# A transformer layer's front: parts, row loads and early projections dealt anew over the engines, the first rows loaded in three stages

## What is computed

```python
def _layernorm(x, axis=-1, eps=1e-05):
    m = jnp.mean(x, axis=axis, keepdims=True)
    v = jnp.var(x, axis=axis, keepdims=True)
    return (x - m) / jnp.sqrt(v + eps)
...
        q = x @ Wq.T + bq
        k = x @ Wk.T + bk
        v = x @ Wv.T + bv
...
        q, k, v = (split(q), split(k), split(v))
        scores = jnp.einsum('bhqd,bhkd->bhqk', q, k) / jnp.sqrt(jnp.float32(HEAD_DIM))
        if CAUSAL:
            mask = jnp.tril(jnp.ones((seq, seq), bool))
            scores = jnp.where(mask, scores, jnp.float32(NEG))
        attn = jax.nn.softmax(scores, axis=-1)
        out = jnp.einsum('bhqk,bhkd->bhqd', attn, v)
        out = out.transpose(0, 2, 1, 3).reshape(batch, seq, D_MODEL)
        return out @ Wo.T + bo
...
        logits = x @ gate_w.T
        top_v = jnp.max(logits, axis=-1)
        sel = jnp.argmax(logits, axis=-1)
        rw = jax.nn.sigmoid(top_v)
        out = jnp.zeros_like(x)
        n_exp = gate_w.shape[0]
        for e in range(n_exp):
            mask = (sel == e).astype(x.dtype)
            xs = x * (rw * mask)[:, None]
            g = xs @ w_gate[e].T
            u = xs @ w_up[e].T
            out = out + u * jax.nn.silu(g) @ w_down[e].T
        return out.reshape(b, s, h)
    x = L0_attn_x
    x = x + _L0_attn_ref(_layernorm(x, axis=-1), ...)
    x = x + _L0_ffn_ref(_layernorm(x, axis=-1), ...)
    return x
```

## Time and profile before

| | before |
|---|---|
| median of 3 runs (lowest to highest) | 519.79 us (519.75 to 520.91) |
| the profiled execution | 519.78 us, span 518.1 |
| busy share of the span | PE 95%, DVE 85%, ACT 73%, POOL 44% |
| granted TensorE clock, mean | 0.989 |
| first lead piece, first turn, first score product of unit 0 | 31.90, 43.65, 58.25 us |

### The profile page before, as it was taken

The page is one execution under the profiler, slowest core; times in us unless marked ns, Lnnn a source line. Parts: engine busy times, 40 slices in busy tenths (PEclk is TensorE's granted clock), DMA queues, the critical chain, the costliest instruction groups (busy, mean ns, idle before and its releaser), DMA issues.

```text
span 518.1 us, 12773 instructions
## 1 busy us (share of the span) xinstructions
PE 493.8 (95%) x4797; PEld 219.9 (42%) x4797; DVE 442.3 (85%) x695; ACT 375.8 (73%) x790; POOL 225.5 (44%) x526
## 2 busy tenths in 40 slices
PE   8699799999999999999999999999999999999997
PEld 7555333243333324333343333334332346777764
DVE  5958789999999999999999989999998358888864
ACT  7245598988889888898988889898888972223321
POOL 5398165363544536344463634446244242222200
PEclk9899999999999999999999999999999999999999
DMA  6251023323202341220234112021130212222001
GB/s 176 48 149 63 4 66 73 101 65 101 73 7 74 84 103 53 48 74 8 75 85 108 50 29 76 10 76 41 46 95 7 74 42 67 61 63 62 20 22 40
DMA packets 33550, 32.63 MB, mean 63 GB/s; under 512 B 10448, under 2 KB 26960, under 8 KB 33488
## 3 DMA queue, kind: packets, MB, share of 16 engines
q1 hardware_dynamic: 33376, 31.48, 23.0%
q10 hardware_dynamic: 112, 0.33, 0.2%
HBM read 20.26 MB, written 11.01 MB: 60 GB/s over the span
## 4 chain that ended last, share of the span: by engine, by line
PE 62%; DVE 28%; ACT 4%; POOL 3%; issue 2%; ACTq 0%; POOLq 0%; DVEq 0%
PE ps L1201 19%; DVE top_p L900 10%; PE ps L1185 10%; PE ps L1146 8%; DVE top_p L895 7%; DVE top_p L897 6%; PE ps L1268 6%; PE ps L1254 5%; PE ps L1259 5%; POOL xn L574 2%; ACT sum_sb L769 2%; DVE top L916 2%; PE ps L1154 1%; PE ps L1230 1%; ACT prob L778 1%
## 5 line engine op out<-in xcount | busy, mean ns | idle before, releaser
L778 ACT ACTIVATE prob<-ps 128x512 f32<-128x512 f32 (+2 forms) x640 | 303.4, 564 | 33.4 <-PE ps L1185 32.2
L655 POOL TENSOR_SCALAR_AFFINE_SELECT prob<-prob 128x256 f32<-128x256 f32 x256 | 99.6, 416 | 176.9 <-ACT prob L778 173.9
L1185 PE MATMUL ps<-q_rows,k_rows 51*128 51x512 bf16 (+3 forms) x768 | 169.7, 329 | 1.2 <-ACT gate_x L733 1.0
L895 DVE TENSOR_REDUCE top_p<-ps 128x2 f32<-128x1024 f32 x128 | 151.0, 1221 | 9.6 <-PE ps L1146 8.6
L1201 PE MATMUL ps<-prob,v_all 128*9 128x512 f32 (+3 forms) x1536 | 157.7, 491 | 1.4 <-POOL prob L655 0.2
L1146 PE MATMUL ps<-k_rows,q_rows 48*128 48x128 bf16 (+3 forms) x1024 | 113.7, 266 | 7.5 <-DVE top_p L900 4.4
L1185 PEld LDWEIGHTS ps<-q_rows,k_rows 51*128 51x128 bf16 x768 | 53.4, 94 | 145.5 <-ACT prob L778 128.1
L900 DVE TENSOR_REDUCE top_p<-ps 128x8 f32<-128x1024 f32 x64 | 76.7, 1220 | 10.8 <-PE ps L1154 10.3
L897 DVE TENSOR_REDUCE top_p<-ps 128x4 f32<-128x1024 f32 x64 | 75.4, 1216 | 2.7 <-PE ps L1146 2.7
L1146 PEld LDWEIGHTS ps<-k_rows,q_rows 48*128 48x128 bf16 x1024 | 45.6, 94 | 27.0 <-DVE top_p L900 8.9
L1201 PEld LDWEIGHTS ps<-prob,v_all 128*9 128x9 f32 x1536 | 24.5, 88 | 51.5 <-issue 30.9
(11 more groups left out here) (110 smaller groups left out, 453.4 us busy)
## 6 DMA issues: line engine op xcount, KB each, us to landing
split_parts<-part SPq DMA_DIRECT2D x12, 384.0 KB, 4.4
q_rows<-split_parts SPq DMA_DIRECT2D x31, 96.0 KB
k_rows<-split_parts SPq DMA_DIRECT2D x31, 96.0 KB
value_sums<-sum_sb SPq DMA_DIRECT2D x128, 18.0 KB
x_sb<-x SPq DMA_DIRECT2D x8, 256.0 KB, 4.5
qk<-value_sums SPq DMA_DIRECT2D x8, 256.0 KB, 3.8
qk<-inverse_sums SPq DMA_DIRECT2D x8, 256.0 KB, 4.1
out<-y SPq DMA_DIRECT2D x8, 256.0 KB, 2.3
```

The lines of the kernel that those rows point to most:

```text
L655: last = g.affine_select(out=quarter, in_=quarter, pattern=[[0, GH], [1, Q]], base=Q * (1 - z), channel_multiplier=-1, compare_op=ALU.is_g ...
L778: a.activation(prob[:, i % NB, g0:g0 + heads, 0:cols], ps[:, load_at(u, n) % 3, 0:heads * cols].rearrange("p (s t) -> p s t", s=heads), AC ...
L895: return v.tensor_reduce(top_p[:, c, place, s:s + 3:2, m], banks, AX.X, ALU.max)
L1185: last = mm(ps[:, l % 3, m * cols:(m + 1) * cols], k_rows[rows, k, j // TPH, s + m, j % TPH * P:(j % TPH + 1) * P], q_rows[rows, k, c, s + ...
```

## The change

- ScalarE casts part 0 of half (0,1), DVE makes both halves' third parts, and GpSimd none.
- Unit 0's parts leave one by one, twelve stores in place of four (`send_first`), each part with a semaphore of its own (`first_out`).
- Unit 0's rows are loaded in three stages (`load_first`): stage 0 (the q rows of part 0 in three copies, and the k rows with one part) on GpSimd's queue, once part 0 has landed; stage 1 on SyncE; stage 2 on SyncE and ScalarE, two DMAs each.
- xn of half (1,0) goes from DVE to ScalarE, as x times rstd plus a shift (minus mean times rstd) that GpSimd computes.
- xn_t of (1,1), v of (1,0), q and k of (1,1) are copied out of PSUM by DVE in place of ScalarE; steps 6 and 7 are measured after that.
- GpSimd raises rstd of steps 6 and 7 after it has scaled batch 2; its memset of v_all stands earlier, that of ramp later.
- The bias products stand in the front between two runs of `keep_busy` (12 and 12 in place of 36) and read b_v and b_oc broadcast in place.
- `AHEAD` is 8: v of (1,1) stands before the first piece.

```diff
@@ -121,7 +121,7 @@
     EARLY += [("v", *half)] if half == (1, 1) or not after else [("xn_t", *after), ("v", *half)]
     if half == (1, 1):
         EARLY.append(("xn_t", *after))
-AHEAD = 7
+AHEAD = 8
...
+        def load_first(eng, n, rg):
+
+            loaded = rows_in[0] if n else first_in
+            load_queries(eng, 0, rg, *PART_ROWS[n], loaded)
+            load_keys(eng, 0, rg, *PART_ROWS[2 - n], loaded)
+
+        def rows_loaded(u):
+
+            return 192 * (u // 3 + 1) - (0 if u % 3 else 64)
 
...
@@ -392,10 +410,17 @@
...
+            def send_first(h, n0, n1):
+                for s in range(2):
+                    for n in range(n0, n1):
+                        sp.dma_start(split[:, n, 0:1, :, :, h, s, :].rearrange("e u d r t -> (u d r) e t"),
+                                     part[64 * s:64 * s + 16, h, :, n, :]).then_inc(first_out[n], 16)
+
...
@@ -410,17 +435,32 @@
...
-            for h in range(2):
-                send_parts(0, h, range(0, 1))
-            for h in range(2):
-                sp.wait_ge(split_out[h], 32)
+            sp.wait_ge(first_part[0], 1)
+            send_first(0, 0, 1)
+            sp.wait_ge(first_part[1], 1)
+            send_first(1, 0, 1)
+            sp.wait_ge(first_part[0], 2)
+            send_first(0, 1, 2)
+            sp.wait_ge(part3_set[0], 1)
+            send_first(0, 2, 3)
+            sp.wait_ge(first_part[1], 2)
+            send_first(1, 1, 2)
+            sp.wait_ge(part3_set[1], 1)
+            send_first(1, 2, 3)
             sp.wait_ge(k_rows_set, 1)
-            load_rows(0)
-            sp.wait_ge(rows_in[0], 192)
+
+            for n in range(2):
+                sp.wait_ge(first_out[n], 64)
+            load_first(sp, 1, 0)
+            load_first(sp, 1, 1)
+            sp.wait_ge(first_out[2], 64)
+            load_first(sp, 2, 0)
+            sp.wait_ge(first_in, 64)
+            sp.wait_ge(rows_in[0], rows_loaded(0))
             for h in range(2):
                 send_parts(0, h, range(1, UPB))
             for h in range(2):
-                sp.wait_ge(split_out[h], 64)
+                sp.wait_ge(split_out[h], 32)
             load_rows(1)
             send_top(0, 0)
...
@@ -554,16 +594,16 @@
...
+            g.memset(v_all[:, :, :, :, HD:HD + 1], 1.0).then_inc(v_ones_set, 1)
             rsqrt1(2, 2)
-            pool.wait_ge(part2_set, 1)
-            g.tensor_tensor(part[:, 0, :, 2, :], rest[:, 0, :, :], part[:, 0, :, 1, :],
-                            ALU.subtract).then_inc(part3_set[0], 1)
-            g.memset(v_all[:, :, :, :, HD:HD + 1], 1.0).then_inc(v_ones_set, 1)
-            for e in range(EXPERTS):
-                last = g.memset(ramp[:, :, e:e + 1], float(EXPERTS - e))
-            last.then_inc(const_set, 2)
+            pool.wait_ge(rstd_set, 3)
+            chain.link(g.tensor_tensor(shift[:], moments1[:, 2, :, 0], rstd1[:, 2, :], ALU.mult))
+            g.tensor_scalar(shift[:], shift[:], -1.0, None, ALU.mult).then_inc(shift_set, 1)
+            pool.wait_ge(k_rows_set, 1)
+            pool.wait_ge(first_out[0], 64)
+            load_first(g, 0, 0)
+            load_first(g, 0, 1)
             rsqrt1(4, 2)
-            rsqrt1(6, 2)
...
             scale(2)
+            rsqrt1(6, 2)
             scale(3)
...
+            for e in range(EXPERTS):
+                last = g.memset(ramp[:, :, e:e + 1], float(EXPERTS - e))
+            last.then_inc(const_set, 2)
             split_top(0, 0)
...
@@ -746,6 +790,8 @@
             for h in range(2):
                 copy_side(0, h, 0)
                 copy_side(0, h, 1)
+            act.wait_ge(qk_set[1], 2)
+            a.activation(part[:, 1, :, 0, :], qk[:, 0, 1, :, :], ACT.Copy).then_inc(first_part[1], 1)
             act.wait_ge(centre_mm, 1)
             a.activation(w_v[:, DIM:], ps[:, 0, 0:EXPERTS], ACT.Copy).then_inc(w_v_set, 1)
...
@@ -754,13 +800,20 @@
...
-            for e in EARLY[:1]:
+            act.wait_ge(shift_set, 1)
+            act.wait_ge(turned[0], 1)
+            for i in range(TPH):
+                last = a.activation(xn[:, 0, i, :], x_sb[:, 2 * TPH + i, :], ACT.Identity,
+                                    bias=shift[:, i:i + 1], scale=rstd1[:, 2, i:i + 1])
+            last.then_inc(xn_set[0], 1)
+            for e in EARLY[:3]:
                 take(e)
-            for h in range(2):
-                act.wait_ge(split_out[h], 32)
             act.wait_ge(k_rows_set, 1)
-            load_half(act, 0, 1, PART_ROWS[:2])
-            for e in EARLY[1:]:
+            for n in range(3):
+                act.wait_ge(first_out[n], 64)
+            load_first(act, 2, 1)
+
+            for e in EARLY[7:]:
                 take(e)
...
@@ -847,44 +900,74 @@
...
             def take_parts(h):
                 dve.wait_ge(qk_set[h], 2)
-                chain.link(v.tensor_copy(part[:, h, :, 0, :], qk[:, 0, h, :, :]))
+                if h == 0:
+                    v.tensor_copy(part[:, h, :, 0, :], qk[:, 0, h, :, :]).then_inc(first_part[h], 1)
+                dve.wait_ge(first_part[h], 1)
                 chain.link(v.tensor_tensor(rest[:, h, :, :], qk[:, 0, h, :, :], part[:, h, :, 0, :],
                                            ALU.subtract))
-                second = v.tensor_copy(part[:, h, :, 1, :], rest[:, h, :, :])
-                if h == 0:
-                    second.then_inc(part2_set, 1)
-                else:
-                    chain.link(second)
-                    v.tensor_tensor(part[:, h, :, 2, :], rest[:, h, :, :], part[:, h, :, 1, :],
-                                    ALU.subtract).then_inc(part3_set[h], 1)
+                v.tensor_copy(part[:, h, :, 1, :], rest[:, h, :, :]).then_inc(first_part[h], 1)
+                dve.wait_ge(first_part[h], 2)
+                v.tensor_tensor(part[:, h, :, 2, :], rest[:, h, :, :], part[:, h, :, 1, :],
+                                ALU.subtract).then_inc(part3_set[h], 1)
 
...
             measure(2)
             measure(3)
             take_parts(0)
             take_parts(1)
-            scale(1, 0)
-            scale(1, 1)
-            dve.wait_ge(bias_in, 16 * 4)
-            v.tensor_copy(xs[:, 0, 0, :], b_v[:].to_broadcast((P, DIM)))
-            v.tensor_copy(xs[:, 0, 1, :], b_oc[:].to_broadcast((P, DIM))).then_inc(wide_set, 1)
-            for n in range(4, STEPS):
-                measure(n)
+            scale(3)
+            dve.wait_ge(bias_mm, 1)
+            v.tensor_tensor(b_o[:], b_o[:], ps[:, 4, 0:DIM], ALU.add)
+            v.tensor_copy(b_gate[:], ps[:, 4, DIM:WIDE]).then_inc(bias_set, 1)
+
+            def copy_side(b, h, side):
+                dve.wait_ge((q_mm, k_mm)[side][h], b + 1)
+                v.tensor_scalar(qk[:, b, h, side, :], ps[:, 1 + side, :], b_qk[:, side:side + 1], None, ALU.add
+                                ).then_inc(qk_set[h], 1)
+
+            def copy_xn(b, h):
+                dve.wait_ge(turned[h], b + 1)
+                dve.wait_ge(v_mm[h], b)
+                tokens = xn_t[:, h, :].rearrange("p (m e t) -> p m e t", e=2, t=Q)
+                v.tensor_copy(tokens[:, :, 1, :], ps[:, 0, 0:HALF // 2].rearrange("p (m t) -> p m t", t=Q))
+                v.tensor_copy(tokens[:, ::-1, 0, :], ps[:, 0, HALF // 2:].rearrange("p (m t) -> p m t", t=Q)
+                              ).then_inc(xn_t_set[h], 1)
+
+            def copy_v(b, h):
+                dve.wait_ge(v_mm[h], b + 1)
+                at = wide(v_banks(b, h))
+                tile = b * (2 * TPH) + h * TPH
+                for z in range(2):
+                    v.tensor_copy(v_all[:, b, h * TPH + 2 * z:h * TPH + 2 * z + 2, :, 0:HD],
+                                  at[:, z, :, 0:DIM].rearrange("p j (g d) -> p j g d", d=HD))
+                v.tensor_copy(gate_x[:, tile:tile + TPH, :].rearrange("p (z j) e -> p z j e", z=2), at[:, :, :, DIM:]
+                              ).then_inc(v_set[h], 1)
+
+
+            assert EARLY[3:7] == [("xn_t", 1, 1), ("v", 1, 0), ("q", 1, 1), ("k", 1, 1)]
+            measure(4)
+            measure(5)
+            copy_xn(1, 1)
+            copy_v(1, 0)
+            copy_side(1, 1, 0)
+            copy_side(1, 1, 1)
+            measure(6)
+            measure(7)
             dve.wait_ge(top_low_set, 1)
 
...
@@ -939,10 +1022,6 @@
             for e in LEAD:
                 if e[0] in ("piece", "turn"):
                     take(e)
-                if e == ("piece", 0, 0):
-                    dve.wait_ge(bias_mm, 1)
-                    v.tensor_tensor(b_o[:], b_o[:], ps[:, 1, 0:DIM], ALU.add)
-                    v.tensor_copy(b_gate[:], ps[:, 1, DIM:WIDE]).then_inc(bias_set, 1)
...
@@ -1092,8 +1171,6 @@
                     turn1(b, h, 0).then_inc(turned[h], 1)
                 elif kind == "q":
                     pe.wait_ge(qk_set[1 - h if n else 0], 2 * (b + h) - 1)
-                    if n == 2:
-                        pe.wait_ge(bias_set, 1)
...
@@ -1115,13 +1192,21 @@
             project_v(0, 1).then_inc(v_mm[1], 1)
```

(13 more changed lines are left out.)

60 lines of the change are left out of this document (30 added, 30 removed).

## The result

The changed kernel takes 517.16 us, the median of six runs (516.05 to 519.34), beside 519.83 (519.35 to 520.91) for the kernel before, run beside it: a ratio of 0.995, with a 95% interval of 0.9934 to 0.9967. That is 2.7 us less; 3.0 were forecast, and 516.8 us. The profiled execution took 516.74 us, with a span of 515.0.

The account below looks back on a forecast made before the run. The prediction took GpSimd's gapless row before the first turn, then TensorE's serial list to S, as the bound on unit 0's start. Terms -1.9, -1.4 and +0.3 sum to -3.0: 516.8 us, range 514.9 to 518.8.

Parts of the forecast that it names:

- the two large terms: Unit 0's start: the first turn 1.9 us earlier, and the list from that turn to S 1.4 us shorter.
- DVE's head: DVE's steps before GpSimd's first raise: both halves in 7.15 us, ending at 19.8, so GpSimd starts at 23.8.
- S: TensorE's first score matmul of unit 0, at 58.25 us before the change, forecast at 55.0.
- GpSimd's row sets the turn: GpSimd's raises, 16 scalings, memsets and split before TensorE's first turn: turn at 41.8 instead of 43.65, -1.9 us.
- The DMAs on GpSimd's queue: Four row-load issues before GpSimd's first raise: 1.1 us each, covered by 5.1 us of waiting, zero in the sum.
- rivals 1 and 2: GpSimd's DMAs delay the head: 1, up to 7.1 us, 523.9 (chance 0.11); 2, partial slip, 517.4 to 518.8 (0.16).
- AHEAD = 8: TensorE between turn and S: one projection (1.06 us) moves before the turn, last piece (0.32) fills a wait; -1.4 us.
- Given back in unit 0: Behind S: the last piece's reduction and join on DVE end later, delaying TensorE's next piece; +0.3 us.
- TensorE's front: TensorE before the turn: first piece at 29.5, DVE's reductions done at 39.9, under 41.8; staged loads pay zero.
- 3 (DVE sets the turn): If GpSimd's scalings took 0.65 instead of 0.78, DVE's 39.9 would set the turn: 514.9 us; chance 0.07.
- 4 (the clock stays low in the front): TensorE's first piece comes 2 us later, moments 6 and 7 are 0.7 late for GpSimd: 517.5 us; chance 0.09.
- 5 (no shift survives): The first units swallow the shift, held by a store or load of SyncE's: 519.5 us; chance 0.07.

Follow-up runs that it names:

- The second group of runs: The changed kernel run once more, unaltered, beside its variants and the kernel before: 517.69 us over nine runs, ratio 0.9949.
- ScalarE's scaling: Changed kernel with xn of half (2,0) made by ScalarE instead of GpSimd and the ramp memsets behind the split: 514.88 us, ratio 0.9902.
- the three kernels with late rows: Changed kernel with unit 0's old stores and row loads (519.33 us), the same with 36 useless products before the first piece (516.84), or stage 0 on SyncE (518.91).
- the two kernels with fill: Changed kernel with useless products in three idle places of unit 0 (516.65 us), and that with 24 more ahead of the first turn (515.04).
- the old loads: Changed kernel with unit 0's parts in four stores and rows loaded by SyncE (eight DMAs) and ScalarE (four), none by GpSimd: 519.33 us, ratio 0.9979.

## Why the prediction was right, and where not

The mechanism was right for the two large terms. That the number came out so close is in part luck. In the profiled execution 0.4 us of scatter at the start and 0.4 us more than worked out in DVE's head stand against 0.6 us more given back behind S. The second group of runs has 2.3 us instead of 2.7. And the medians of the changed kernel hold time at half clock that no term priced.

**GpSimd's row sets the turn: right.** Forecast 18.0 us from its first raise to the turn, measured 17.96; the half microsecond put in front of the split came out at the turn as 0.47.

**DVE's head: right, a little better than worked out.** The cast came at 12.21 and its steps for the two halves ended at 19.28, so 7.07 for the 7.15 of the sum; the parts of 1.22 and 1.23 are in the table to 0.01. The rest up to GpSimd's start was 3.8 instead of 4.0. What made the difference of 3.04 long, GpSimd's subtraction beside it, is shown by the run that gives GpSimd its subtraction back: 3.08. The shares of ScalarE's cast and of the four scalings rest on rows alone.

**The DMAs on GpSimd's queue: right that they are covered; the size was below the value taken.** Bounds 1.2 to 12.2 us for the four, taken 4.4, measured 0.84 + 0.56 + 0.60 + 0.54 = 2.5, begun at 19.11 where 18.7 was worked out, and 1.39 us of cover left. The first two stood beside DVE's four scalings (19.20 to 20.31) and show nothing of the 3.06 that I allowed. In the second execution of the changed kernel they began at 17.78, beside DVE's cast and subtraction, and took 0.84, 0.56, 0.60 and 0.68. And the kernel without these four starts its raise at the same time. So rivals 1 and 2 fall. What the Trainium skill states (SBUF — State Buffer, section on SBUF's two separate sides), 3100 ns for such a DMA overlapped with DVE, is not borne out here: the issues took 0.54 to 0.84 us, and the whole of one, issue to landing, 2.7 to 2.8 in the profiled execution. The page speaks of a DVE copy in a two-port mode, and no run here tells whether these DVE steps hold the port as that one does.

**AHEAD = 8: right.** 13.22 us from the turn to S (13.2 forecast), and 14.60 with `AHEAD` at 7. This holds at full clock: 14.80 and 15.30 were seen in executions whose clock fell behind the turn. It holds too only while TensorE waits for GpSimd at the turn, as the prediction has it: where it reaches the turn without a wait, it waits 0.47 or 0.49 us for DVE behind it, and the stretch takes 13.8 us (ScalarE's scaling, and the three kernels with late rows).

**Given back in unit 0: right in mechanism, wrong in size.** Forecast 0.3, measured 0.93 in the first execution and 0.16 in the second (460.01 against 459.85). The second turn stands at S + 2.52 instead of S + 2.31, which is the queue of DVE that I described, 0.2 us. The rest, 0.7, is TensorE's half clock, which begins at 56.8 us instead of 62 and lasts longer, and covers the first value products, from 59.43. The other executions bear this out: without half clock, in the two kernels with fill, it is 458.5 us from S to the end; with a shortfall of 1.7 it is 459.85 before and 460.0 in the changed kernel's second execution; with 3.4 it is 460.8. What the kernel before would be if it were filled was not tried.

**TensorE's front: "zero, with 1.9 us to spare" was wrong.** The times of its front hold: xn was there at 19.59 (19.8 forecast), the turn of (1,0) came at 19.74 (20.2), the clock stayed at 1.00 from 20 to 30 us, and the first piece came at 28.54 (29.5). What failed is the conclusion that the loads in stages pay nothing as there are 1.9 us to spare. I let the first piece slip in thought and kept the clock and the turned tiles where they were. With the old loads TensorE waits 2.53 us idle, gets 1.2 GHz for some 3.5 us and makes GpSimd wait 1.51 for a tile to be turned; turn 1.9 us late, and a ratio of 0.9979 where the changed kernel has 0.9949 and 0.995. The intervals overlap, so the loss in the time is likely rather than shown; the lateness at the turn is shown. With stage 0 on SyncE's queue the clock is low for some 10 us, and the time 518.91. The spare time was right for a delay by itself (0.7 us of 2.6 came through when the wait was filled), not for a delay during which TensorE stands idle. The bound behind it was misread as well. DVE's join is not behind seven further pieces, at 39.9, but behind the fifth piece, at 36.06, as in the kernel before (40.08). What comes next behind GpSimd is TensorE's list, at 39.1, as ScalarE's scaling shows.

**Rivals.** 3 (DVE sets the turn) did not come: TensorE waited 1.88 us for GpSimd, and DVE's bound in it rested on the misread join. 4 (the clock stays low in the front) did not either, but its mechanism is what the runs are about, at other places. 5 (no shift survives) fell with the result.

**What stays open.** Whether a wait of 1.9 us ahead of the turn is followed by a half clock differed between executions of one and the same kernel (it was in two of three profiled ones, and behind 2.25 us in a fourth); so did the length of the half clock behind S. No run here tells what decides it. So the median of the changed kernel holds a loss that the forecast priced at zero, about as large as the gain: 517.69 us in one group, and 515.04 in another with the idle time filled.

## What to carry to other kernels

A wait of TensorE's of 2 us can cost almost as much again as its length where dense work follows (here 1.5 us behind one of 1.9): read the granted clock of the windows behind each such wait, in several executions, and price a slip of the work ahead of it with the clock and not by the spare time alone. Where the engine that holds the path is a side engine with a gapless row, give a piece of it to another engine, here four scalings of GpSimd's to ScalarE (1.9 us at the turn), and check at what point the next one takes over. Two elementwise engines that meet on large tiles can cost more than the work that was to be shared: in the kernel before, a subtraction of 1.23 us was kept off DVE at a price of 1.8 (3.04 for 1.22).

## What the runs showed of the hardware

- Over all profiled executions GpSimd's issues of unit 0's row loads took 0.54 to 0.88 us, SyncE's 0.29 to 0.86 and ScalarE's 0.55 to 1.47; that GpSimd's are no dearer I had not expected.
- GpSimd's operations on 128x4 elements at 13.55 and 14.31 took 0.67 us each, while DVE ran a difference and a cast; a raise's first step on 128x8 takes 0.24. It looks like the hindrance of the long difference once more; that wasn't tried by itself.
- A memset of 128x512 took 0.52 us where the elements lie together, and 1.02 for v_all, where every ninth is written.
- The stretches at half clock behind idle time lasted some 3.5 us (behind the turn, and behind S in the kernel before), 7 (behind S in the changed kernel) and 10 (in the front, with stage 0 on SyncE's queue), and did not come in every execution: 514.69 to 519.03 us for one kernel on one chip, 515.0 to 515.15 with its idle time filled.
